# Linear attention: turned queries copied amid the curves, first projections in idle banks, and half of each head's sum made on GpSimd

## The reference

```python
q, k, v = heads(x @ Wq.T), heads(x @ Wk.T), heads(x @ Wv.T)
g = sigmoid(x @ Wg.T + bg)
qf, kf = softplus(q) * (g + 1e-6), softplus(k)
kv_cum = cumsum(kf[..., :, None] * v[..., None, :], axis=tokens)
z_cum = cumsum(kf, axis=tokens)
num = einsum('bhtd,bhtde->bhte', qf, kv_cum)
den = einsum('bhtd,bhtd->bht', qf, z_cum) + 1e-6
out = (num / den) @ Wo.T
```

## Time and profile before

| | before |
|---|---|
| median of 3 runs (lowest, highest) | 1916.31 us (1915.63, 1920.72) |
| profiled execution | 1912.57 us, span 1910.8 us |
| PE, DVE, ACT, POOL busy | 93%, 76%, 52%, 69% |
| mean granted clock of TensorE | 0.957 |
| linear attention, from barrier to barrier | about 1481 to 1690 us of the span |

### The profile page before, as it was taken

One profiled execution on the slowest core, in us unless ns is written; L12 is line 12 of the kernel. 1 busy time (PEld: TensorE's weight loads), 2 busy tenths in 40 slices (PEclk: granted clock), 3 DMA queues, 4 the chain that ended last, 5 costly groups with the idle time before them and its releaser, 6 DMA issues. The chain is left out here.

```text
span 1910.8 us, 32627 instructions
## 1 busy us (share of the span) xinstructions
PE 1769.3 (93%) x11830; PEld 1292.3 (68%) x11830; DVE 1448.1 (76%) x2497; ACT 992.8 (52%) x1970; POOL 1309.7 (69%) x1327
## 2 busy tenths in 40 slices
PE   6999999999999999999999999959997578849998
PEld 4777767776767776767776767648885355538886
DVE  7777777777777777777777777559998166768998
ACT  3544434454445444444443444437887555437776
POOL 1777667767776677676766776839998244617998
PEclk9999999999999999999999999969998588969999
DMA  3000000000000000000000000000000000000000
GB/s 90 1 1 1 2 1 1 2 1 2 1 1 1 2 1 1 1 1 1 1 1 1 1 1 1 23 22 2 1 1 1 7 1 1 1 1 7 12 13 17
DMA packets 15088, 10.88 MB, mean 6 GB/s; under 512 B 433, under 2 KB 14546, under 8 KB 14930
## 3 DMA queue, kind: packets, MB, share of 16 engines
q1 hardware_dynamic: 14930, 8.80, 1.6%
HBM read 6.70 MB, written 2.10 MB: 5 GB/s over the span
## 5 line engine op out<-in xcount | busy, mean ns | idle before, releaser
L1244 DVE TENSOR_REDUCE attn_neg<-attn_shared 128x2 f32<-128x1024 f32 x512 | 611.6, 1222 | 263.0 <-PE attn_shared L1377 262.2
L1127 ACT ACTIVATE attn_prob<-attn_shared 128x1024 f32<-128x1024 f32 x288 | 295.1, 1026 | 369.1 <-PE attn_shared L1406 368.9
L1039 POOL TENSOR_TENSOR attn_row_sum<-attn_row_sum,attn_prob 128x1024 f32<-128x1024 f32 (+3 forms) x256 | 416.1, 1625 | 24.2
L497 ACT ACTIVATE experts_weighed<-experts_y,kept_gate 128x128 f32<-128x128 f32 x1024 | 278.4, 408 | 63.9 <-PE experts_y L724 49.7
L1016 POOL TENSOR_TENSOR attn_prob<-attn_prob,attn_below 128x256 f32<-128x256 f32 x256 | 188.4, 736 | 133.4 <-ACT attn_prob L1127 133.4
L580 DVE SCALAR_TENSOR_TENSOR experts_acc<-experts_y,kept_gate,experts_acc 128x128 f32<-128x128 f32 x960 | 261.4, 340 | 12.1 <-PE experts_y L724 10.1
L1034 POOL TENSOR_TENSOR attn_row_sum<-attn_prob 128x1024 f32<-128x1024 f32 x64 | 135.7, 2120 | 171.5 <-ACT attn_prob L1127 169.0
L1373 PE MATMUL attn_shared<-attn_qk_hi 64*128 64x512 f32 x1024 | 230.6, 429 | 8.5 <-DVE attn_neg L1244 5.5
L1263 DVE RECIPROCAL attn_den<-attn_den 128x256 f32<-128x256 f32 x128 | 214.7, 1719 | 13.4 <-ACT attn_den L1151 13.4
L1377 PE MATMUL attn_shared<-attn_qk_hi,attn_qk_lo 64*128 64x512 f32 x1024 | 213.0, 393 | 0.0
L1375 PE MATMUL attn_shared<-attn_qk_lo,attn_qk_hi 64*128 64x512 f32 x1024 | 212.0, 391 | 0.0
(11 more groups left out here) (227 smaller groups left out, 3371.2 us busy)
## 6 DMA issues: line engine op xcount, KB each, us to landing
kept_x<-in_L_attn_a_x_dram SPq DMA_DIRECT2D x4, 512.0 KB, 8.5
out_dram<-kept_x SPq DMA_DIRECT2D x8, 256.0 KB, 2.3
attn_prob<-in_L_attn_a_Wkv_dram SPq DMA_DIRECT2D x2, 512.0 KB, 6.1
kept_half_raw<-_ffn_expert_weights_dram SPq DMA_DIRECT2D x2, 512.0 KB, 4.5
last_other_half<-_ffn_expert_weights_dram SPq DMA_DIRECT2D x2, 512.0 KB, 4.6
attn_prob<-in_L_attn_a_Wq_dram SPq DMA_DIRECT2D x1, 512.0 KB, 4.6
attn_wo<-in_L_attn_a_Wo_dram SPq DMA_DIRECT2D x1, 512.0 KB, 5.8
attn_bo<-in_L_attn_a_bo_dram SPq DMA_DIRECT2D x1, 64.0 KB, 5.8
```

What stands on the lines that cost most here:

```text
L497: ins = act.activation(weighed[n][:, e, :], y[fill(pair, quad, odd) % RING][:, e * D:(e + 1) * D], ACT.Copy, scale=k.gate[:, c, quad * PER ...
L1039: pool.tensor_tensor(row_sum[n][:, :, at:], row_sum[n][:, :, at:], src, ALU.add).then_inc(add_ok, 1)
L1127: act.activation(prob[n % RING][:, :, :], buffer((p, t))[:, :, :], ACT.Exp).then_inc(exp_ok, 1)
L1244: dve.tensor_reduce(neg[p % 2][:, :, b, half], buffer((p, b, half))[:, :, :], AX.X, ALU.max, negate=True).then_inc(max_ok, 1)
```

## The change

- ACT loads the sigmoid's table with a small activation (`warm`) as its first instruction of the stage.
- `bank(n)`: the projections of chunks 0 to 5 go to the six banks of `cum`, 6 to `z`, 7 to the first bank of `cum` again (it waits for the copies of chunk 0), and from 8 on all to `z`.
- ACT makes the q copy of a group between exp and ln of the next group's curves, and `floor` after the first pair of copies of a step.
- GpSimd `fold` adds, in each head, products 4 to 7 onto products 0 to 3, in place; DVE's `add_up` waits for it and reduces four instead of eight. DVE does the sum and carried part of chunk n-1 after product and state of chunk n; `soften` moves to the place of chunk 0 and `invert` to that of chunk 1.
- PE's order within a step: one stretch of sums or carried parts lies between any two projections, `turn_o` and `out` come one stretch later, around the last sums.

```diff
@@ -1512,7 +1512,7 @@
...
         pick_raw, pick = sb("pick_raw", [P, P]), sb("pick", [P, P], F32R)
-        upto, own = sb("upto", [P, P]), sb("own", [P, HEADS])
+        upto, own, warm = sb("upto", [P, P]), sb("own", [P, HEADS]), sb("warm", [P, 1])
@@ -1536,7 +1536,7 @@
...
         o_turned, oT_ok, y_ok, x_ok, gate_step = (sem(n) for n in ("o_turned", "oT_ok", "y_ok", "x_ok", "gate_step"))
-        sum_ok = sem("sum_ok")
+        sum_ok, half_ok = sem("sum_ok"), sem("half_ok")
@@ -1553,6 +1553,11 @@
...
             return n - n // (PER_BATCH * GROUP)
+
+        def bank(n):
+            if n < 6:
+                return cum[n // 3][:, n % 3 * 512:(n % 3 + 1) * 512]
+            return cum[0][:, 0:512] if n == 7 else z[:, :]
@@ -1594,6 +1599,13 @@
...
 
+            def fold(g, c):
+                n = g * GROUP + c
+                pool.wait_ge(prod_ok, n + 1)
+                have = prod[n % 2][:, :, :].rearrange("p e (h d) -> p (e h) d", d=DH)
+                pool.tensor_tensor(have[:, :, 0:DH // 2], have[:, :, 0:DH // 2], have[:, :, DH // 2:DH],
+                                   ALU.add).then_inc(half_ok, 1)
+
@@ -1614,17 +1626,24 @@
...
                     outer(g, 0)
+                if exists(g - 1):
+                    fold(g - 1, 3)
+                if exists(g):
                     outer(g, 1)
+                    fold(g, 0)
                     outer(g, 2)
+                    fold(g, 1)
...
                     outer(g, 3)
+                    fold(g, 2)
...
         def _(act):
+            act.activation(warm[:, :], k.eps[:, :], ACT.Sigmoid)
@@ -1639,11 +1658,11 @@
...
                     act.wait_ge(soft_ok, g - 1)
-                act.activation(raw[g % 2][:, c, :], z[:, 0:3 * D], ACT.Copy).then_inc(raw_ok, 1)
+                act.activation(raw[g % 2][:, c, :], bank(n)[:, 0:3 * D], ACT.Copy).then_inc(raw_ok, 1)
...
                     act.wait_ge(added_ok, updates(GROUP * (g - 2)))
-                act.activation(v[g % 3][:, c, :, 0:DH], z[:, 3 * D:4 * D].rearrange("p (h e) -> p h e", e=DH),
+                act.activation(v[g % 3][:, c, :, 0:DH], bank(n)[:, 3 * D:4 * D].rearrange("p (h e) -> p h e", e=DH),
@@ -1657,6 +1676,8 @@
...
                 act.activation(log[:, :, :], log[:, :, :], ACT.Exp, scale=-1.0).then_inc(log_step, 1)
+
+            def logarithm(g):
@@ -1677,17 +1698,22 @@
...
                 g = s - 2
-                if exists(g):
-                    q_out(g)
+                if exists(s):
+                    projected(s, 0)
...
                 if exists(s):
-                    for c in range(GROUP):
-                        projected(s, c)
+                    projected(s, 1)
+                    projected(s, 2)
+                    projected(s, 3)
...
                     curves(s)
+                if exists(g + 1):
+                    q_out(g + 1)
+                if exists(s):
+                    logarithm(s)
@@ -1714,10 +1740,11 @@
...
                 n = g * GROUP + c
-                dve.wait_ge(prod_ok, n + 1)
+                dve.wait_ge(half_ok, n + 1)
...
                     dve.wait_ge(o_ok, g - 1)
-                dve.tensor_reduce(num[g % 2][:, c, :, :], prod[n % 2][:, :, :].rearrange("p e (h d) -> p e h d", d=DH),
+                dve.tensor_reduce(num[g % 2][:, c, :, :],
+                                  prod[n % 2][:, :, :].rearrange("p e (h d) -> p e h d", d=DH)[:, :, :, 0:DH // 2],
@@ -1754,13 +1781,14 @@
...
                             new_state(n + 1)
-                    if c == 0 and exists(g - 1):
+                    have = (g, c - 1) if c else (g - 1, 3)
+                    if exists(have[0]):
+                        add_up(*have)
+                        if not begins(have[0] * GROUP + have[1]):
+                            add_carried(*have)
+                    if c == 1 and exists(g - 1):
                         invert(g - 1)
-                    if exists(g):
-                        add_up(g, c)
-                        if not begins(n):
-                            add_carried(g, c)
-                    if c == 1 and exists(s - 1):
+                    if c == 0 and exists(s - 1):
@@ -1777,11 +1805,16 @@
...
             def project(g, c):
-                rows = slice((g * GROUP + c) * P, (g * GROUP + c + 1) * P)
-                pe.matmul(z[:, :], k.xT_hi[:, rows], wT_hi[:, :], start=True, stop=False)
-                pe.matmul(z[:, :], k.xT_lo[:, rows], wT_hi[:, :], start=False, stop=False)
-                pe.matmul(z[:, :], k.xT_hi[:, rows], wT_lo[:, :], start=False, stop=False)
-                pe.matmul(z[:, 0:D], pick[:, :], bg[:, :], start=False, stop=True).then_inc(z_ok, 1)
+                n = g * GROUP + c
+                rows, to = slice(n * P, (n + 1) * P), bank(n)
+                if n == 7:
+                    pe.wait_ge(v_ok, 1)
+                if n >= 8:
+                    pe.wait_ge(v_ok, n)
+                pe.matmul(to[:, :], k.xT_hi[:, rows], wT_hi[:, :], start=True, stop=False)
+                pe.matmul(to[:, :], k.xT_lo[:, rows], wT_hi[:, :], start=False, stop=False)
+                pe.matmul(to[:, :], k.xT_hi[:, rows], wT_lo[:, :], start=False, stop=False)
+                pe.matmul(to[:, 0:D], pick[:, :], bg[:, :], start=False, stop=True).then_inc(z_ok, 1)
@@ -1844,28 +1877,25 @@
...
                 if exists(s):
-                    if s:
-                        pe.wait_ge(v_ok, GROUP * s)
...
                     add_state(g, 0)
-                if exists(s):
-                    pe.wait_ge(v_ok, GROUP * s + 1)
-                    project(s, 1)
-                if exists(g):
...
                 if exists(s):
-                    pe.wait_ge(v_ok, GROUP * s + 2)
-                    project(s, 2)
+                    project(s, 1)
...
                 if exists(s):
-                    pe.wait_ge(v_ok, GROUP * s + 3)
+                    project(s, 2)
+                if exists(g):
+                    within(g, 2)
+                if exists(s):
...
                 if exists(g):
-                    within(g, 2)
+                    carried(g, 2)
+                    add_state(g, 2)
@@ -1875,12 +1905,10 @@
...
                 if exists(g):
-                    carried(g, 2)
-                    add_state(g, 2)
+                    within(g, 3)
...
                 if exists(g):
-                    within(g, 3)
```

## The result

The changed kernel takes 1941.3 us (1938.2 to 1943.8), the one before 1916.0 (its median with one more run than in the table above): a ratio of 1.0129 with a 95% interval of 1.0102 to 1.0155. It is slower by 25 us; forecast were 37, and the range (1924 to 1978) holds it. The profiled execution took 1939.4 us, its span is 1937.7 against 1910.8.

The account below looks back on a forecast made before the run. No engine is full; a chain of hand-overs sets the pace. Profiled: 1912.6 - 15.1 + 26.9 + 0.85 = 1925.2, plus 24.6 for the clock = 1949.8; as median 1953 us, range 1924 to 1978.

Parts of the forecast that it names:

- The start: Up to product (0,1): more banks, the early sigmoid table and the earlier q copy were to gain 15.1 us.
- Fold and reduction: GpSimd's fold of 576 pairs was to take 1.40 us, DVE's reduction 0.75 us instead of 1.34.
- The turns: Product (0,1) to (7,3): PE's next sums wait for DVE's late sum, so both alternate; 175.9 us against 149.0, loss 26.9.
- The end: At the stage's last chunk, the last sum waits for its fold: 0.85 us more.
- The clock: PE's idle stretches bring its clock to half for a third of the work: 24.6 of 73.7 us added.
- Rival B: PE and DVE take turns but PE's clock holds: 1929 us, from 1924 to 1939; chance 0.25.
- the ring: Chain of hand-overs through curves, q copy, projection, sums and queries that sets the 22.2 us of a step.
- `floor` costs nothing: ACT's `floor` between a step's first two copies waits for product 0, 3 us before the next projection is ready: no cost.

Follow-up runs that it names:

- The run with the clock kept up: The changed kernel with one or two groups of sums matmuls made twice in PE's idle time before the wait for the late sum: 1924.4 us.
- the split release: The changed kernel, but the first two matmul groups of `within` wait only for the product of two chunks back, the third for the late sum: 1912.2 us.
- the sum ahead of the product: The changed kernel with its fold, but DVE does the sum and carried part of chunk n-1 ahead of the product of chunk n: 1916.3 us.
- the sum in place: The changed kernel without the fold, and with each chunk's sum and carried part right behind its own product: 1900.2 us.
- the late sum without a fold: The changed kernel without `fold`: DVE reduces all eight products, still only after the next chunk's product: 1967.8 us.

## Why the prediction was right

**The start** (gain 15.1 us). Product (0,1) began at 1516.33 against 1531.24, with the stage's first DVE instruction 0.64 us later than before: 15.6. The first four copies were 1.5 us apart, as the clock stayed at half for four projections (I had two); the projection and the sums ahead of product (0,1) ran at full clock and made it good. The early table and that product, in ACT's and DVE's timelines:

```profile
1482.07 1.28 ACT L1646 ACT_TABLE_LOAD   x1 [1.01 <-PEq L369]
...
1516.33 1.36 DVE L1738 TENSOR_TENSOR linear_prod<-linear_cum,linear_q 128x1152 f32<-128x1152 f32 x1 [0.40 <-PE linear_cum L1856]
```

**Fold and reduction** (1.40 and 0.75): 1.40 and 0.74.

**The turns** (175.9 us at full clock against 149.0). The run with the clock kept up took 174.8, the changed kernel 191.8. This step carried the forecast, and the runs show it from three sides: the split release (-29), the sum ahead of the product (-25), the sum in place (-68, against the late sum without a fold).

**The end** (0.85 more): product (7,3) to the last `into_x` took 10.25 us (1708.05 to 1718.30), against 9.38: 0.87.

**The clock** (24.6 us, a third of the work at half clock) is the term that was mis-sized: 191.8 - 174.8 = 17.0 us by the traces, 17 by the medians. Of the 30 sums after product (0,1), 12 took over 2.9 us; but most projections and carried parts behind them ran at full clock again, so of 73.7 us not a third but a little under a quarter fell due. The third was a guess between none and all of it; that it came this near is in part luck. Rival B's price (1929, no falls) came out as 1924.4 when the clock was kept up: its size was right, its condition was not met. The rule that the prediction cites from the Trainium skill (TensorE: Matmul & The Clock Gate, "HAM oscillation"), by which only longer gaps bring the clock down, did not hold here: it fell with gaps of 2.54 us and less (the sums at 1638.36).

**What is left of the difference.** The profiled execution was forecast 37 us longer and was 27 longer. Of these 10 us the clock is 7.6 and the turns 1.1 (174.8 instead of 175.9). Another 1.8 lie behind the stage: from the end of the last `into_x` to the end of the span, where the kernels are the same, it took 218.7 instead of 220.5 us, and no run shows why.

**What I left out.** I read the q copy as the end of the ring, worth 2.4 us a step. Alone it was worth 5 us in all; the softplus's place, which I listed as moved and did not price, was worth 19.5. And "`floor` costs nothing" fits the changed kernel, where GpSimd waits only 3.2 us in all for `invert`, but with `invert` it costs 26 us once the turns are gone (GpSimd waits 74.4 us in the run with the sum in place). The same goes for the fold: I looked at GpSimd's total, and not at what stands behind a fold in its order. None of this changed the forecast; that the turns hid it fits these waits, but I had not reasoned so, and it was luck.

## What to carry to other kernels

When an edit puts work of chunk n-1 behind work of chunk n, look for what that work releases: a double buffer whose release comes one chunk late works like a single one, and two engines begin to take turns. Idle stretches of an engine that waits in turns can bring its clock down on top. And of a change that is slower as a whole, run the parts: here start, q copy and early softplus were worth 37 us; the late sum lost most, and behind it the late `floor` (26 us) and the fold (16 us) lost too, which showed only when the sum was in time again. What a part is worth depends on which wait ends last around it: the fold won 26 us in one order and lost 16 in the other.

## What the runs showed of the hardware

- DVE's softplus reads two operands from SBUF; alone it took 1.22 us. Where it and a GpSimd instruction ran at the same time, the one that began second took longer. In the run with the sum ahead of the product a fold began 0.05 us before it, and the softplus took 2.44 us, to 1.07 us behind the fold's end; the outer product that began while the softplus ran took 3.36 us instead of 2.38. In the changed kernel the softplus mostly began first and took 1.43 us, and the outer product beside it again 3.36. Where it began just behind an outer product, in other steps of the run with the sum ahead of the product, the softplus took up to 3.36 us. The rows are from that run, at the fold:

```profile
1578.50 1.42 POOL L1606 TENSOR_TENSOR linear_prod<-linear_prod 128x576 f32<-128x576 f32 x1 [2.03 <-DVE linear_prod L1738]
1579.87 3.36 POOL L1597 TENSOR_TENSOR linear_kv<-linear_soft,linear_v 128x1152 f32<-128x1152 f32 x1
...
1578.55 2.44 DVE L1773 SCALAR_TENSOR_TENSOR linear_soft<-linear_raw,linear_log 128x1024 f32<-128x1024 f32 x1
```

The Trainium skill (GPSIMD Engine Reference, "Specifications") names contention for SBUF between the two engines when DVE's instruction has two SBUF inputs; the trace agrees. The products, with one input in PSUM, took 1.36 us beside GpSimd as without it (in the kernel before, 1552.88 beside an outer product and 1531.24 with GpSimd idle).
- TensorE's clock was at half after idle stretches of 1.31 to 2.54 us in the changed kernel, and at full after others of the same length, as these two from its timeline show; length alone did not decide:

```profile
1587.78 2.18 PE L1845 MATMUL linear_cum<-linear_kv,linear_upto 128*128 128x512 f32 x6 [2.54 <-issue]
...
1593.79 3.87 PE L1845 MATMUL linear_cum<-linear_kv,linear_upto 128*128 128x512 f32 x6 [1.31 <-issue]
```
